# Attention with rings of three PSUM banks for scores and exponents, and its slots unrolled

## The chip, the core and the metric

The kernel runs on one core of a Trainium2 chip. The metric is the device time of one execution in microseconds (us), as the median of several runs. The engines have names in the profile: PE is TensorE (PEld its weight loads), DVE is VectorE, ACT is ScalarE, POOL is GpSimd, and SP is SyncE, whose queue issues the transfers. PSUM, the memory that TensorE writes, has eight banks of 512 f32 values in each of 128 partitions.

## What is computed

Two layers, each of cross attention and a feed-forward part, over 8 batches of 512 rows and 256 features. Both attentions have 16 heads of 16 features:

```
scores = einsum('bqhd,bkhd->bhqk', qp, kp) / sqrt(16)        # layer 0: masked by the mask
scores = where(mask == 0, -10000., scores)                   # layer 1: only j < i is kept
attn   = softmax(scores, axis=-1)
ctx    = einsum('bhqk,bkhd->bqhd', attn, vp) @ Wo.T + Wo_b
```

Layer norms and residuals stand between them. Layer 0 ends with a ternary matmul on quantized rows, layer 1 with a gated feed-forward on quantized rows. Only the two attentions bear on the change.

## The kernel before

The program has four stages: the projections (`project_phase`), the attention of layer 0, that of layer 1 (both `attention_phase`), and the gated feed-forward. The change is in `attention_phase` alone.

An attention is cut into 32 **slots** (8 batches times `G` = 4 groups of four heads) of 16 **steps** `s`. A slot `t` is a software pipeline over three head groups. In step `s` of slot `t` TensorE makes

- one tile of scores of group `t + 2` (`maxima`, L775), from which VectorE takes the negated row maximum (L1161);
- one tile of transposed scores of group `t` with the maximum already subtracted by extra contraction rows (`exponents`, L798), of which ScalarE takes the exponential into `probs` (L986);
- after every fourth step the product of four heads' `probs` with the values (`weigh`, L820), which accumulates in the bank `av`.

At step 5 the maxima of group `t + 1`, split by GpSimd into three bf16 parts (L1052 to L1058), are transposed by TensorE into the bank `max` (`turn_max`, L830). ScalarE copies them out at its step 8 (L998) and SP writes them by DMA into row positions of `q_stack` (L693), for the exponents of the next slot. At step 10 the finished output of group `t - 1`, which ScalarE copied from `av` at step 4 (L992), is transposed into the bank `turn` (`turn_out`, L839). VectorE normalizes it at its step 13 (L1167, L1171).

In layer 1 the tiles are causal. A query tile needs 128, 256, 384 or 512 keys, and each score tile gets a small mask matmul (L778, L801). Narrow tiles share a bank: four of 128 or two of 256 make one **fill**, which is read by one instruction. In layer 0 each step is a fill of its own.

PSUM is shared out as two score banks, two exponent banks, `av`, `turn`, `max` and `work`. TensorE may write fill `n` of the scores when fill `n - 2` has been read, and likewise for the exponents:

```
n = FILLS * t + f
if place == 0 and not (known(t) and n < 2):
    pe.wait_ge(score_read, n - 1)
```

Each engine runs its own instruction stream in order. Within one step the order on TensorE is `maxima`, `exponents`, `weigh`, `turn_max` or `turn_out`, then the after-work of an earlier batch. That after-work (`after`, `queries`, through the bank `work`) is: output projection and residual in the slot that `behind` numbers j = 0, layer norm on VectorE in j = 1, and in layer 0 also the query projection of layer 1 for the batch before (`queries`, L904) in j = 1, the ternary matmul in j = 2 and a second layer norm in j = 3. In layer 1, slots j = 2 and j = 3 have none.

The slots are run by `run`: those from -2 to 11 are written out, 12 to 27 are a hardware loop (`Fori`) of two passes of eight slots, with semaphore values computed in registers (`wait_apart`), and 28 to 40 are written out again.

Of the kernel before, what the change touches and what calls it, by code (L numbers as in the profile page):

```python
# [12 lines left out]
P = 128  # L13
# [11 lines left out]
NSTACK = R_MAX + PARTS  # L25
VW = HD + 1
# [477 lines left out]
def attention_phase(nc, dram, scratch, const, w, layer, stacks, normed=None, tops=None, ffn=None):  # L504
# [22 lines left out]
    with ExitStack() as mem:  # L527
# [52 lines left out]
        out_copied, out_turned, out_normed = sem("out_copied"), sem("out_turned"), sem("out_normed")  # L580
        inverted = sem("inverted")
        max_chain, max_split = sem("max_chain"), sem("max_split")
        max_turned, max_copied = sem("max_turned"), sem("max_copied")
# [83 lines left out]
        def _(sp):  # L667
# [18 lines left out]
            def slot(t, r, i):  # L686
                half, g = (r // G) % 2, r % G
                if there(t, t + 1):
                    u = r + 1
                    wait_apart(sp, max_copied, t + 2)  # L690
# [4 lines left out]
                if not (known(t) and not RING - LEAD <= t <= LAST_LEAD):  # L695
                    n = r + LEAD
                    wait_apart(sp, exp_full, FILLS * (t + LEAD - RING + 1))
# [61 lines left out]
        def _(pe):  # L759
            def program(general):  # L760
                def maxima(t, r, i, s):
# [23 lines left out]
                def exponents(t, r, i, s):  # L785
# [5 lines left out]
                    n = FILLS * t + f  # L791
                    if place == 0 and not (known(t) and n < 2):
                        pe.wait_ge(exp_done, n - 1)
                    q0 = P * kc if causal else 0
                    w = T - q0
                    o = exp_bank[(FILLS * r + f) % 2][:, place * w:(place + 1) * w]
# [13 lines left out]
                def weigh(t, r, i, kc):  # L810

                    half, g = (r // G) % 2, r % G
                    pe.wait_ge(exp_done, FILLS * t + fills_through(kc))
# [10 lines left out]
                def turn_max(t, r):  # L824

                    pe.wait_ge(max_split, t + 1)
                    if not (known(t) and t < 1):
                        pe.wait_ge(max_copied, t)
                    for qt in range(TT):
                        mm = pe.transpose(max_bank[0:PARTS * 4, qt * P:(qt + 1) * P], max_parts[r % 2][:, qt, :, :].rearrange("p a b -> p (a b)"), const["ident_b"][:, :])  # L830
# [983 lines left out]
```

## Time and profile before

| | us |
|---|---|
| median of 3 runs (lowest, highest) | 1672.05 (1665.68, 1674.05) |
| the profiled execution | 1669.25 |
| its span, first to last instruction | 1667.5 |
| slots 1 to 32 of layer 0, from copy to copy of L992 | 477.4 |
| slots 1 to 32 of layer 1, likewise | 402.3 |

A slot is read off the trace from one start of ScalarE's copy `b_out<-b_av` (L992) to the next, since it comes once in a slot. A matmul's own duration overlaps its neighbours': the time that TensorE needs for one is the distance to the next start where nothing is waited for. Durations of VectorE and ScalarE likewise overlap by about 0.1 us where instructions follow each other directly.

### The profile page before, as it was taken

To read this page: it belongs to the slowest core of one execution; us is meant where nothing else is said; L and a number is where in the kernel's file an instruction comes from. 1 tells how busy PE (TensorE), PEld (TensorE's weight loads), DVE (VectorE), ACT (ScalarE), POOL (GpSimd) and SP (SyncE) were. 2 spreads that over 40 slices of the span, in tenths; PEclk is the share of its full clock that TensorE was granted. 3 is DMA by queue.
4 is the path that set the end of the run, shared out by engine and by line. 5 is a ranking of instruction groups with operands and counts; after the bars stand their busy time and mean duration, and the time that the engine had idled before them with its cause. 6 is when DMAs were issued, how large, how long until landed. Compare 5 with 4: busy or idle time off the path is not lost. (4 is left out here: it accounts for less than half of the span.)

```text
span 1667.5 us, 24772 instructions
## 1 busy us (share of the span) xinstructions
PE 1394.5 (84%) x7817; PEld 671.1 (40%) x7829; DVE 1053.0 (63%) x2019; ACT 869.7 (52%) x1488; POOL 219.9 (13%) x335
## 2 busy tenths in 40 slices
PE   8898946999999999997468999998998599970199
PEld 4444411232433433432224554454444344430187
DVE  5434226789889889884367667775674342997832
ACT  4444422766767767765215555554555244868331
POOL 0000000011121221222200000000000000445100
PEclk9999975999999999998759999999999799995599
DMA  7757455123243332333030243233330000315122
GB/s 270 258 187 259 175 167 157 40 85 90 61 114 85 97 116 72 108 103 115 32 102 2 55 115 98 85 86 85 99 83 27 13 0 0 151 76 189 63 89 88
DMA packets 87926, 170.85 MB, mean 102 GB/s; under 512 B 14585, under 2 KB 49156, under 8 KB 86276
## 3 DMA queue, kind: packets, MB, share of 16 engines
q1 hardware_dynamic: 87812, 169.42, 32.0%
q8 instruction: 60, 0.98, 0.3%
q14 instruction: 54, 0.44, 0.1%
HBM read 108.27 MB, written 60.31 MB: 101 GB/s over the span
## 5 line engine op out<-in xcount | busy, mean ns | idle before, releaser
L1161 DVE TENSOR_REDUCE b_neg_max<-b_score 128x1 f32<-128x512 f32 (+3 forms) x864 | 554.0, 665 | 226.1 <-PE b_score L778 127.8
L986 ACT ACTIVATE b_probs<-b_exp 128x512 f32<-128x512 f32 (+1 forms) x864 | 478.3, 582 | 363.6 <-PE b_exp L801 196.3
L775 PE MATMUL b_score<-k_stack,q_stack 97*128 97x512 bf16 (+3 forms) x1024 | 366.2, 359 | 85.9 <-DVE b_neg_max L1161 43.4
L798 PE MATMUL b_exp<-q_stack,k_stack 100*128 100x512 bf16 (+3 forms) x1024 | 352.2, 347 | 22.4 <-DMA q_stack<-b_max_rows 11.6
L775 PEld LDWEIGHTS b_score<-k_stack,q_stack 97*128 97x128 bf16 x1024 | 100.8, 99 | 383.4 <-DVE b_neg_max L1161 276.6
L820 PE MATMUL b_av<-b_probs,values 128*17 128x512 f32 (+3 forms) x2048 | 229.2, 520 | 0.8 <-ACT b_probs L986 0.6
L1687 PE MATMUL f_down<-f_w_downT,f_tmp 128*128 128x256 f32 x384 | 85.9, 388 | 88.4 <-DVE f_tmp L1369 88.4
L1052 POOL CAST b_max_parts<-b_neg_max 128x16 bf16<-128x16 f32 x64 | 14.5, 227 | 1027.4 <-DVE b_neg_max L1161 1027.4
L798 PEld LDWEIGHTS b_exp<-q_stack,k_stack 100*128 100x128 bf16 x1024 | 100.3, 99 | 103.8 <-ACT b_probs L986 40.3
L778 PE MATMUL b_score<-diag_qk,minus_big 128*128 128x128 bf16 x512 | 116.8, 229 | 0.0
L1687 PEld LDWEIGHTS f_down<-f_w_downT,f_tmp 128*128 128x128 f32 x384 | 74.8, 195 | 99.9 <-DVE f_tmp L1369 89.2
L801 PE MATMUL b_exp<-diag_kq,minus_big 128*128 128x128 bf16 x512 | 113.3, 223 | 0.0
L1405 PE MATMUL f_bank<-normed,f_w_upT 128*128 128x512 f32 x192 | 84.2, 595 | 1.1 <-ACT f_up L1472 1.0
L1405 PE MATMUL f_bank<-normed,f_w_gateT 128*128 (+1 forms) x192 | 84.3, 596 | 0.0
L423 DVE TENSOR_TENSOR a_va<-a_bank,bv 128x512 f32<-128x512 f32 x32 | 22.0, 686 | 84.8 <-PE a_bank L261 84.7
L853 PE MATMUL b_work<-wo,b_attendedT 128*128 128x256 f32 x256 | 65.2, 400 | 3.1 <-DVE b_x L1119 1.7
L998 ACT ACTIVATE b_max_rows<-b_max 12x512 bf16<-12x512 bf16 x64 | 36.5, 570 | 59.1 <-PE b_max L830 59.1
L333 ACT ACTIVATE a_part_q<-a_bank 128x512 bf16<-128x512 f32 x48 | 26.8, 594 | 75.1 <-PE a_bank L243 58.7
L241 PE MATMUL a_bank<-a_ctxT,wk 128*128 128x512 f32 x128 | 60.5, 617 | 5.6 <-DMA bk<-L_bk_in 5.5
L1361 ACT ACTIVATE f_tmp<-f_hidden,f_magic,f_inv_prod 128x768 f32 (+2 forms) x32 | 30.2, 1016 | 65.6 <-PE f_down L1687 42.0
L820 PEld LDWEIGHTS b_av<-b_probs,values 128*17 128x17 f32 x2048 | 34.0, 95 | 73.2 <-issue 45.6
L1504 DVE TENSOR_REDUCE f_tops_gate<-f_hidden (+1 forms) x8 | 26.8, 3354 | 57.4 <-ACT f_hidden L1444 57.4
(206 smaller groups left out, 1822.2 us busy)
## 6 DMA issues: line engine op xcount, KB each, us to landing
q_stack<-s_q SPq DMA_DIRECT2D x384, 64.0 KB
s_k<-a_part_k SPq DMA_DIRECT2D x48, 256.0 KB, 4.3
k_stack<-s_k SPq DMA_DIRECT2D x64, 192.0 KB
s_up<-f_up SPq DMA_DIRECT2D x6, 1536.0 KB, 5.1
s_va<-a_va SPq DMA_DIRECT2D x16, 544.0 KB, 4.2
values<-s_va SPq DMA_DIRECT2D x16, 544.0 KB, 3.9
a_mask_q<-mask_in SPq DMA_DIRECT2D x8, 1024.0 KB, 7.4
k_stack<-s_k SPq DMA_DIRECT2D x64, 128.0 KB
```

The costliest lines, as they stand in the source:

```text
L241: mm = pe.matmul(o[:, :], w["w" + n][:, c, m * P:(m + 1) * P], src[:, c, :], start=(c == 0), stop=(c == DC - 1))
L775: mm = pe.matmul(o, q, KS[half][0:R_MAX, h, 0:w], start=True, stop=not general)
L778: mm = pe.matmul(o[:, w - P:w], const["minus_big"][:, :], d[:, :], start=False, stop=True, skip_group_check=True)
L798: mm = pe.matmul(o, k, QS[half][0:NSTACK, h, q0:T], start=True, stop=not general)
L801: mm = pe.matmul(o[:, 0:P], const["minus_big"][:, :], d[:, :], start=False, stop=True, skip_group_check=True)
L820: mm = pe.matmul(av_bank[32 * j:32 * j + VW, q0:T], VA[half][:, kc, 4 * g + j, :], probs[kc][:, j, q0:T], start=(kc == 0), stop=(kc == TT ...
L853: mm = pe.matmul(work[:, x * D:(x + 1) * D], src[:, c, y * P:(y + 1) * P], wt[:, c, :], start=(c == 0), stop=(c == DC - 1))
L986: nc.scalar.activation(probs[kc][:, h0:h0 + m, q0:T], exp_bank[(FILLS * r + f) % 2][:, 0:m * w].rearrange("p (h n) -> p h n", h=m), ACT.Ex ...
L998: nc.scalar.activation(max_rows[u % 2][:, :], max_bank[0:PARTS * 4, 0:T], ACT.Copy).then_inc(max_copied, 1)
L1161: nc.vector.tensor_reduce(neg_max[u][:, qt, h0:h0 + m], score_bank[(FILLS * r + f) % 2][:, 0:m * w].rearrange("p (h n) -> p h n", h=m), AX ...
L1405: mm = pe.matmul(bank[f][:, :], wt[:, c, f * P:(f + 1) * P], xT[:, bass.ds(b, 1), c, :].rearrange("p a n -> p (a n)"), start=(c == 0), sto ...
L1687: mm = pe.matmul(down[2 * half + u][:, j, :], od[half][:, f, t * P:(t + 1) * P], w_downT[:, f, :], start=(f == 0), stop=(f == FC - 1))
```

## The change

1. **Rings of three.** The banks `turn` and `max` go. Scores and exponents get three banks each, and TensorE may write fill `n` when fill `n - 3` has been read.
2. **The transposes become fills.** The transposed maxima are a fill of the exponent ring, issued at step 5 as before and copied out by ScalarE at its step 5 where it was step 8. The transposed outputs are a fill of the score ring, issued at step 10 as before and normalized by VectorE at its step 10 where it was step 13. The semaphores `max_turned`, `max_copied`, `out_turned` and `out_normed` are replaced by counts of `exp_full`, `exp_done`, `score_full` and `score_read`.
3. **Unrolled slots.** All slots from -2 to 40 are written out; every wait is on a constant.

The arithmetic, the number and the shapes of the instructions stay. In `exponents` the same edit as in `maxima` is made with `exp_fill`, `exp_done` and `exp_bank`.

```diff
+RINGS = 3
...
-        score_bank = [pb(f"score{i}", [P, T], F32) for i in range(2)]
-        exp_bank = [pb(f"exp{i}", [P, T], F32) for i in range(2)]
+        score_bank = [pb(f"score{i}", [P, T], F32) for i in range(RINGS)]
+        exp_bank = [pb(f"exp{i}", [P, T], F32) for i in range(RINGS)]
         av_bank = pb("av", [P, T], F32)
-        turn_bank = pb("turn", [P, T], F32)
-        max_bank = pb("max", [P, 2 * T], BF16)
...
+        SLOTS = range(-2, LAST + 10)
+        TURN_MAX, TURN_OUT = 5, 10
+
         def run(eng, slot):
 
-            for r in range(-2, 12):
-                slot(r, r, 0)
-            with eng.Fori(1, NB // 2 - 1) as i:
-                for r in range(4, 12):
-                    slot(8 * i + r, r, i)
-            for r in range(4, 17):
-                slot(LAST - 7 + r, r, NB // 2 - 1)
+            for t in SLOTS:
+                slot(t, t, 0)
+
+        score_fill, exp_fill = {}, {}
+        for t in SLOTS:
+            for s in range(STEPS):
+                f, place, m = fill_of(MAX_FILLS, s)
+                if place == 0 and 0 <= t + 2 <= LAST:
+                    score_fill["max", t + 2, f] = len(score_fill)
+                if s == TURN_OUT and 0 <= t - 1 <= LAST:
+                    score_fill["out", t - 1] = len(score_fill)
+                f, place, m = fill_of(EXP_FILLS, s)
+                if place == 0 and 0 <= t <= LAST:
+                    exp_fill["exp", t, f] = len(exp_fill)
+                if s == TURN_MAX and 0 <= t + 1 <= LAST:
+                    exp_fill["max", t + 1] = len(exp_fill)
...
                 def maxima(t, r, i, s):
...
-                    n = FILLS * t + f
-                    if place == 0 and not (known(t) and n < 2):
-                        pe.wait_ge(score_read, n - 1)
+                    n = score_fill["max", t, f]
+                    if place == 0 and n >= RINGS:
+                        pe.wait_ge(score_read, n - RINGS + 1)
                     w = widths[qt]
-                    o = score_bank[(FILLS * r + f) % 2][:, place * w:(place + 1) * w]
+                    o = score_bank[n % RINGS][:, place * w:(place + 1) * w]
...
                 def turn_max(t, r):
 
+                    n = exp_fill["max", t]
                     pe.wait_ge(max_split, t + 1)
-                    if not (known(t) and t < 1):
-                        pe.wait_ge(max_copied, t)
+                    if n >= RINGS:
+                        pe.wait_ge(exp_done, n - RINGS + 1)
...
-                    mm.then_inc(max_turned, 1)
+                    mm.then_inc(exp_full, 1)
...
                 def turn_out(t, r):
 
+                    n = score_fill["out", t]
                     pe.wait_ge(out_copied, t + 1)
-                    if not (known(t) and t < 1):
-                        pe.wait_ge(out_normed, t)
+                    if n >= RINGS:
+                        pe.wait_ge(score_read, n - RINGS + 1)
...
-                    mm.then_inc(out_turned, 1)
+                    mm.then_inc(score_full, 1)
...
         @block.scalar
...
-                    if s == 8 and there(t, t + 1):
-                        act.wait_ge(max_turned, t + 2)
+                    if s == TURN_MAX and there(t, t + 1):
+                        n = exp_fill["max", t + 1]
+                        act.wait_ge(exp_full, n + 1)
...
         @block.sync
...
-                    wait_apart(sp, max_copied, t + 2)
+                    sp.wait_ge(exp_done, exp_fill["max", t + 1] + 1)
...
         @block.gpsimd
...
-                    pool.wait_ge(max_turned, t)
-                wait_apart(pool, score_read, FILLS * (t + 2))
+                    pool.wait_ge(exp_full, exp_fill["max", t - 1] + 1)
+                pool.wait_ge(score_read, maxima_through(t + 1))
...
         @block.vector
...
-                    if s == 13 and there(t, t - 1):
+                    if s == TURN_OUT and there(t, t - 1):
                         v, g = (r - 1) % 2, (r - 1) % G
-                        got = turn_bank[:, :].rearrange("p (t h e) -> p t h e", t=TT, h=4)
-                        dve.wait_ge(out_turned, t)
+                        n = score_fill["out", t - 1]
+                        got = score_bank[n % RINGS][:, :].rearrange("p (t h e) -> p t h e", t=TT, h=4)
+                        dve.wait_ge(score_full, n + 1)
...
```

ScalarE in layer 0, from the first exponential of query tile group 1 (step 4) of a slot on. Names are tile and buffer number, with the semaphores waited for. Before:

```order
L986 ACTIVATE b0_probs1<-b0_exp0 128x512 [waits b0_av_done,b0_exp_full]
L992 ACTIVATE b0_out1<-b0_av 128x512 [waits b0_out_turned,b0_av_done]
L986 ACTIVATE b0_probs1<-b0_exp1 128x512 [waits b0_exp_full]
L986 ACTIVATE b0_probs1<-b0_exp0 128x512 [waits b0_exp_full]
L986 ACTIVATE b0_probs1<-b0_exp1 128x512 [waits b0_exp_full]
L986 ACTIVATE b0_probs2<-b0_exp0 128x512 [waits b0_av_done,b0_exp_full]
L998 ACTIVATE b0_max_rows1<-b0_max 12x512 [waits b0_max_landed1,b0_max_turned]
L986 ACTIVATE b0_probs2<-b0_exp1 128x512 [waits b0_exp_full]
```

Changed:

```order
L1007 ACTIVATE b0_probs1<-b0_exp1 128x512 [waits b0_av_done,b0_exp_full]
L1013 ACTIVATE b0_out1<-b0_av 128x512 [waits b0_score_full,b0_av_done]
L1007 ACTIVATE b0_probs1<-b0_exp2 128x512 [waits b0_exp_full]
L1020 ACTIVATE b0_max_rows1<-b0_exp0 12x512 [waits b0_max_landed1,b0_exp_full]
L1007 ACTIVATE b0_probs1<-b0_exp1 128x512 [waits b0_exp_full]
L1007 ACTIVATE b0_probs1<-b0_exp2 128x512 [waits b0_exp_full]
L1007 ACTIVATE b0_probs2<-b0_exp0 128x512 [waits b0_av_done,b0_exp_full]
L1007 ACTIVATE b0_probs2<-b0_exp1 128x512 [waits b0_exp_full]
```

The copy to `b0_max_rows` stands two exponentials further ahead and reads a bank of the exponent ring, so that the two exponentials behind it use the two banks that are left.

VectorE in layer 0, around the normalization in the same kind of slot. Before:

```order
L1161 TENSOR_REDUCE b0_neg_max1<-b0_score0 128x1 [waits b0_score_full]
L1161 TENSOR_REDUCE b0_neg_max1<-b0_score1 128x1 [waits b0_score_full]
L1161 TENSOR_REDUCE b0_neg_max1<-b0_score0 128x1 [waits b0_score_full]
L1161 TENSOR_REDUCE b0_neg_max1<-b0_score1 128x1 [waits b0_score_full]
L1167 RECIPROCAL b0_inv_sum0<-b0_turn 128x16 [waits b0_out_turned]
L1171 TENSOR_TENSOR b0_attended0<-b0_turn,b0_inv_sum0 128x4x64 [waits b0_inverted]
L1161 TENSOR_REDUCE b0_neg_max1<-b0_score0 128x1 [waits b0_score_full]
```

Changed:

```order
L1184 TENSOR_REDUCE b0_neg_max1<-b0_score1 128x1 [waits b0_score_full]
L1184 TENSOR_REDUCE b0_neg_max1<-b0_score2 128x1 [waits b0_score_full]
L1191 RECIPROCAL b0_inv_sum0<-b0_score0 128x16 [waits b0_score_full]
L1195 TENSOR_TENSOR b0_attended0<-b0_score0,b0_inv_sum0 128x4x64 [waits b0_inverted]
L1184 TENSOR_REDUCE b0_neg_max1<-b0_score1 128x1 [waits b0_score_full]
L1184 TENSOR_REDUCE b0_neg_max1<-b0_score2 128x1 [waits b0_score_full]
```

The two instructions on the transposed output moved ahead by two reductions, and their operand is now a bank of the score ring, between two fills of it.

## Rows read from the trace of the kernel before

**Rows 1.** The page: the span and the engines' busy time over it.

```profile
span 1667.5 us, 24772 instructions
...
PE 1394.5 (84%) x7817; PEld 671.1 (40%) x7829; DVE 1053.0 (63%) x2019; ACT 869.7 (52%) x1488; POOL 219.9 (13%) x335
```

**Rows 2.** Busy time by stretch: layer 0 without after-work, then j = 0, 1, 2, 3.

```profile
core 0: us, PE busy (x) PEld busy (x) DVE busy (x) ACT busy (x) POOL busy (x), PEclk, DMA share, GB/s
313.12:326.94 13.82, 13.24 (x75) 3.71 (x73) 10.71 (x19) 9.83 (x20) 0.84 (x4) 1.00 0.22 59
543.99:560.92 16.93, 16.75 (x99) 7.81 (x96) 13.23 (x26) 10.83 (x22) 4.88 (x6) 1.00 0.40 123
497.53:514.28 16.75, 16.75 (x91) 6.13 (x88) 15.09 (x41) 12.75 (x26) 3.25 (x5) 1.00 0.27 80
514.28:529.02 14.74, 14.01 (x87) 4.99 (x84) 13.16 (x26) 11.24 (x22) 2.92 (x5) 1.00 0.30 81
529.02:543.99 14.97, 13.71 (x79) 4.14 (x76) 13.75 (x39) 10.32 (x20) 3.77 (x6) 1.00 0.38 107
```

**Rows 3.** The same view, layer 1: written-out slot, j = 0, 1, 2, loop boundary.

```profile
1016.76:1029.00 12.24, 11.39 (x108) 5.66 (x106) 7.35 (x14) 6.66 (x14) 0.83 (x4) 1.00 0.41 102
1041.19:1055.94 14.75, 14.49 (x128) 9.08 (x124) 10.09 (x24) 7.19 (x15) 0.84 (x4) 1.00 0.25 73
1055.94:1068.54 12.60, 11.36 (x108) 5.55 (x105) 11.11 (x31) 6.67 (x15) 0.83 (x4) 1.00 0.37 107
1068.54:1080.76 12.22, 11.30 (x108) 5.60 (x105) 7.28 (x14) 6.66 (x14) 0.83 (x4) 1.00 0.27 72
1120.34:1138.21 17.87, 12.99 (x104) 6.29 (x101) 7.13 (x14) 6.88 (x15) 0.83 (x4) 0.84 0.32 88
```

**Rows 4.** Timeline (start, duration), layer 0: one group of steps on PE.

```profile
319.58 0.38 PE L775 MATMUL b_score<-k_stack,q_stack 97*128 97x512 bf16 x1
...
319.80 0.38 PE L798 MATMUL b_exp<-q_stack,k_stack 100*128 100x512 bf16 x1
...
320.31 0.39 PE L775 MATMUL b_score<-k_stack,q_stack 97*128 97x512 bf16 x1
...
320.91 0.39 PE L775 MATMUL b_score<-k_stack,q_stack 97*128 97x512 bf16 x1
...
321.45 1.05 PE L820 MATMUL b_av<-b_probs,values 128*17 128x512 f32 x8
...
322.43 0.39 PE L775 MATMUL b_score<-k_stack,q_stack 97*128 97x512 bf16 x1
```

**Rows 5.** Timeline, layer 0: runs of reductions and of exponentials without waits between.

```profile
312.41 2.58 DVE L1161 TENSOR_REDUCE b_neg_max<-b_score 128x1 f32<-128x512 f32 x4 [0.81 <-PE b_score L775]
...
323.08 1.09 ACT L986 ACTIVATE b_probs<-b_exp 128x512 f32<-128x512 f32 x2 [0.93 <-PE b_exp L798]
```

**Rows 6.** Timeline of PE, layer 0: after-work, each with what starts next.

```profile
501.06 1.88 PE L904 MATMUL b_work<-b_xT,wq 128*128 128x512 f32 x4
...
502.78 0.38 PE L775 MATMUL b_score<-k_stack,q_stack 97*128 97x512 bf16 x1
...
510.60 0.60 PE L845 MATMUL b_work<-ident_f,b_xn 128*128 128x128 f32 x4
...
511.04 0.38 PE L775 MATMUL b_score<-k_stack,q_stack 97*128 97x512 bf16 x1
```

**Rows 7.** Timeline of PE, layer 1: matmuls that came late.

```profile
1069.57 0.34 PE L798 MATMUL b_exp<-q_stack,k_stack 100*128 100x384 bf16 x1 [0.16 <-ACT b_probs L986]
...
1074.76 0.22 PE L801 MATMUL b_exp<-diag_kq,minus_big 128*128 128x128 bf16 x1
1075.26 0.39 PE L775 MATMUL b_score<-k_stack,q_stack 97*128 97x512 bf16 x1 [0.28 <-DVE b_neg_max L1161]
...
1078.48 0.39 PE L798 MATMUL b_exp<-q_stack,k_stack 100*128 100x512 bf16 x1 [0.26 <-ACT b_probs L986]
```

**Rows 8.** Timeline of PE, layer 1, at the loop's boundary.

```profile
1133.09 0.28 PE L775 MATMUL b_score<-k_stack,q_stack 97*128 97x128 bf16 x1 [4.32 <-issue]
```

More of the change, by code:

```diff
@@ L790, in exponents @@
                     f, place, m = fill_of(EXP_FILLS, s)
-                    n = FILLS * t + f
-                    if place == 0 and not (known(t) and n < 2):
-                        pe.wait_ge(exp_done, n - 1)
+                    n = exp_fill["exp", t, f]
+                    if place == 0 and n >= RINGS:
+                        pe.wait_ge(exp_done, n - RINGS + 1)
                     q0 = P * kc if causal else 0
                     w = T - q0
-                    o = exp_bank[(FILLS * r + f) % 2][:, place * w:(place + 1) * w]
+                    o = exp_bank[n % RINGS][:, place * w:(place + 1) * w]
                     k = KS[half][0:NSTACK, h, kc * P:(kc + 1) * P]
@@ L874, in after @@
                         if n == 0:
-                            pe.wait_ge(out_normed, G * (b + 1))
+                            pe.wait_ge(score_read, score_fill["out", G * (b + 1) - 1] + 1)
                         mm = turn(att[half], n)
@@ L919, in slot @@
                                 weigh(t, r, i, s // 4 - 1)
-                        if s == 5 and there(t, t + 1):
+                        if s == TURN_MAX and there(t, t + 1):
                             turn_max(t + 1, r + 1)
-                        if s == 10 and there(t, t - 1):
+                        if s == TURN_OUT and there(t, t - 1):
                             turn_out(t - 1, r - 1)
@@ L989, in slot @@
                         act.wait_ge(av_done, 4 * t)
-                        if not (known(t) and t < 3):
-                            act.wait_ge(out_turned, t - 2)
+                        if t >= 3:
+                            act.wait_ge(score_full, score_fill["out", t - 3] + 1)
                         nc.scalar.activation(out_sb[(r - 1) % 2][:, :], av_bank[:, :], ACT.Copy).then_inc(out_copied, 1)
-                    if s == 8 and there(t, t + 1):
-                        act.wait_ge(max_turned, t + 2)
+                    if s == TURN_MAX and there(t, t + 1):
+                        n = exp_fill["max", t + 1]
+                        act.wait_ge(exp_full, n + 1)
                         u = r + 1
@@ L1158, in slot @@
                         if place == m - 1:
[L1159 removed]
+                            n = score_fill["max", t + 2, f]
+                            dve.wait_ge(score_full, n + 1)
                             h0, w = s % 4 - place, widths[qt]
[L1161 removed]
+                            nc.vector.tensor_reduce(neg_max[u][:, qt, h0:h0 + m], score_bank[n % RINGS][:, 0:m * w].rearrange("p (h n) -> p h n", h=m),
                                                     AX.X, ALU.max, negate=True).then_inc(score_read, 1)
[L1163 removed]
+                    if s == TURN_OUT and there(t, t - 1):
                         v, g = (r - 1) % 2, (r - 1) % G
[L1165 to L1166 removed]
+                        n = score_fill["out", t - 1]
+                        got = score_bank[n % RINGS][:, :].rearrange("p (t h e) -> p t h e", t=TT, h=4)
+                        dve.wait_ge(score_full, n + 1)
                         nc.vector.reciprocal(inv_sum[v][:, :, :], got[:, :, :, HD]).then_inc(inverted, 1)
@@ L1171, in slot @@
                         nc.vector.tensor_tensor(att[(r - 1) // G % 2][:, :, 4 * HD * g:4 * HD * (g + 1)].rearrange("p t (h d) -> p t h d", h=4),
-                                                got[:, :, :, 0:HD], spread, ALU.mult).then_inc(out_normed, 1)
+                                                got[:, :, :, 0:HD], spread, ALU.mult).then_inc(score_read, 1)
                     if layer == 1 and known(t) and t < 4 and s in (3, 8, 13):
```

26 lines of the change are left out of this document (15 added, 11 removed).

## Prediction

> **What bounds the kernel now.** I read the page first: TensorE is busy for 84% of the span, VectorE for 63%, ScalarE for 52% [rows 1]. Since matmul durations overlap, that does not say that TensorE is full. So I read one slot of each kind as a stretch: in layer 0 a slot without after-work takes 13.82 us with VectorE busy for 10.71 and ScalarE for 9.83, and one of layer 1 takes 12.22 with 7.28 and 6.66 [rows 2, 3]. No engine fills them. The granted clock is 1.00 in both, the upper level of 2.4 GHz, so the clock is not what is lost. Then the timeline of TensorE. Back to back, a 512-column matmul is followed by the next after 0.22 us (319.58 to 319.80) and a `weigh` after 0.98 (321.45 to 322.43) [rows 4]. Next to that stand holes. After the exponent tile at 319.80, which is over at 320.02, the third score tile comes at 320.31: 0.29 lost. The pair from 320.31 is over at 320.75, the fourth score tile comes at 320.91: 0.16 lost. These are waits for a score bank. VectorE does four reductions in a row in 2.58 us, so one each 0.63 (the last lasts 0.69), and two exponentials take 1.09, one each 0.5 [rows 5]. TensorE makes a pair in 0.44, so four pairs outrun VectorE, and it catches up during `weigh`. Two banks are too few for this unevenness, not for the average.
>
> **What a slot needs.** Layer 0: 32 tiles x 0.22 = 7.04, four `weigh` x 0.98 = 3.92, `turn_max` and `turn_out` 0.76 together (four transposes of f32 take 0.44, 510.60 to 511.04 [rows 6]; I take 0.32 for the bf16 ones, an estimate), and about 0.09 before each `weigh` that no bank removes (320.91 plus 0.44 is 321.35, it starts at 321.45 [rows 4]), 0.36. Sum 12.1 of 13.82: 1.7 us of holes in a base slot.
>
> **Part 1, three banks for scores.** Worked for four steps with VectorE at the start idle: tiles at 0, 0.44, 0.88, and the fourth needs the first read, at 0.43 + 0.63 + 0.1 = 1.16, before 1.32. No hole, where it was 0.45. `weigh` ends at 2.83, VectorE's four reductions at 2.96: it is nearly full within a group, and has `turn_out`'s group and `turn_max`'s group to catch up. Its whole work per base slot, 16 x 0.63 + 0.7 = 10.8, stays below 12.1. So all score holes of a base slot go.
>
> **Part 2, the transposes as fills.** The output transpose takes a place in the score ring between the third and fourth tile of its group. VectorE holds that bank for about 0.7 us more. With tiles at 0, 0.44, 0.88, transpose 1.32, fourth tile 1.76, VectorE is through the third at 2.3, the normalization at 3.05, the fourth tile at 3.7; the tile that needs the transpose's bank again comes at 3.7. No hole. The transposed maxima take a place in the exponent ring in the group where ScalarE also copies the output. Its order becomes exponential, output copy, exponential, maxima copy, then two exponentials. The fourth exponent tile of that group needs the second one's bank, which is free after 0.65 + 0.5 + 0.47 + 0.6 = 2.2 us, the same as with two banks and a separate one. So the hole of about 0.3 in this group **stays**: three banks less one fill are two. The same hole stands in layer 1 at 1069.57, with 0.16 shown idle and as much hidden in the modelled durations [rows 7]. This part costs nothing else: GpSimd waits for the same events; SP's wait for the maxima copy stands in the same place of its queue and comes true about 2 us earlier, and the stack transfers queued behind it with it; the DMA engines are busy for 0.22 to 0.41 of a slot [rows 2, 3].
>
> A base slot of layer 0 thus goes from 13.8 to 12.5: **1.3** saved (1.7 less 0.3, and 0.1 for rest). There are four intervals of this kind (slots 1 to 5): 5.2.
>
> **Slots with after-work, layer 0.** j = 1 adds two `turn` (0.88) and two query projections x 1.72 (501.06 to 502.78 [rows 6]), 4.3: needs 16.4 of 16.75, and TensorE is full: 0.4 saved. j = 0 adds as many f32 columns: 16.4 of 16.93, 0.5. j = 2 needs 13.4 of 14.74, but VectorE is busy for 13.16: 1.0. j = 3 needs 12.5 of 14.97, and VectorE is busy for 13.75, with a whole layer norm between reductions: what it can win is its idle 1.2 and one more fill of lead (0.63) less what it leaves idle in any case; I take 1.3 [rows 2]. Seven intervals of the first three kinds and six of the last: 7 x 1.9 + 6 x 1.3 = 21. With the last two intervals (1.5) layer 0 saves **28**.
>
> **Layer 1.** In the slot 1068.54 to 1080.76 late tiles stand six times: from 1069.57 (ScalarE) over 1075.26 (VectorE; the tile before starts at 1074.76 and needs 0.06, so 0.44 lost with 0.28 shown) to 1078.48 (ScalarE) [rows 7]. By their kinds: 1.1 in the two groups with wide score tiles (VectorE), 0.5 in the group with the wide exponents (ScalarE), 0.3 in the `turn_max` group, which stays as above. So a slot without after-work saves 1.6. j = 1 (12.60, VectorE busy 11.11) is bound by VectorE's layer norm for most of its length: 1.0. j = 0 has one hole of 0.4 and small ones: 0.6 [rows 3]. The first four intervals, which share VectorE with the weight quantization, 1.0 each. Sum: 4 + 7 x 0.6 + 7 x 1.0 + 13 x 1.6 + 1.5 = **37.5**.
>
> **Part 3, unrolled.** At the loop's only back edge in layer 1, slot 19 to 20, TensorE stands still for 4.32 us with nothing to wait for, and the matmuls behind it run at a lower clock: that slot took 17.87 us, with a granted clock of 0.84, where its kind takes 12.2 [rows 3, 8]. Without the loop this goes: **5.6**. Straight code costs nothing visible: slots 1 to 11 and 28 on are written out already, and a written-out one takes 12.24 where one in the loop takes 12.22 [rows 3]. The registers' arithmetic was hidden, too, by the same two rows. What I can't see is only whether 43 slots in a row behave as 14 do.
>
> A rule of the Trainium skill speaks against this part. The trace shows that TensorE loses 4.32 us at one jump and none in written-out slots [rows 3, 8]. "Advanced Engine Details and Errata", section "ISA Cache", gives TensorE 128 KB in lines of 256 instructions, with two lines; code that is run once is then fetched line by line, where a loop that fits is kept. By it, unrolling trades one late fetch for many, and if they came late the kernel would be slower; the written-out slots speak for fetches that come in time.
>
> **Sum.** 28 + 37.5 + 5.6 = 71 off the profiled execution's 1669.25: 1598. The median of the runs is 2.8 above that execution, so **1601** for the median. The stages outside the attentions, and the tail of layer 0 after slot 32, stay.
>
> **Rivals.** (a) The third bank gives half. For it: VectorE is busy for 11.11 to 15.09 us in all slots with a norm, and a lead of three fills makes `turn_max` wait for the split maxima, which need the last reduction and four GpSimd steps. Against: base slots have no such work. Then 65 / 2 + 5.6 = 38 off: 1634. (b) The rings give nothing, since the new fills take the third bank's place and what is left is a ring of two: only the back edge goes, and 1666 comes out. For it: that is so in the `turn_max` group. Against: the transposes are one fill in 17 in layer 0 and one in 12 in layer 1. (c) **Slower**: code fetch. If straight code past the first slots stalled as the back edge does, 4.32 us each, then 17 stalls would eat all 71. TensorE runs over 100 matmuls and weight loads in a slot [rows 2]; with a stall in each of the 2 x 16 slots that come out of the loops, 32 x 4.32 = 138 less 71 is 67 more: 1739. Against: [rows 3] as above.
>
> **Chances.** Forecast 0.66, (a) 0.22, (b) 0.07, (c) 0.05. The range is 1588 (VectorE's bound in the norm slots is softer than I took: 1 us more in each of 13) to 1640, which takes in (a). About 0.5% is what a measurement of this kernel can tell from no change; so faster 0.88, same 0.07, slower 0.05.
>
> **What would show it.** Right: a base slot of layer 0 at 12.5 and one of layer 1 at 10.6; four tiles in a row at 0.44 in groups without `turn_max`; the hole before the fourth exponent tile in the `turn_max` group still there; slot 19 to 20 of layer 1 like its neighbours; j = 1 of layer 0 almost unchanged. Wrong: reductions that wait while TensorE waits at `turn_max` (a), holes of the old size (b), or stops with no releaser at places spread over the slots (c).

## The result, and the profile after

The changed kernel takes **1608.9 us** (median of four runs, 1608.38 to 1609.36), beside 1668.97 for the kernel before on the same chip: a ratio of 0.9637, 95% interval 0.9607 to 0.9668. That is 7.9 us above the 1601 forecast and inside its range. The saving is 60.1 us, where 71 was forecast: the kernel before also reads 3.1 us less here than the 1672.05 that the forecast started from. Its profiled execution has a span of 1606.7 us, 60.8 less than before.

The page of the changed kernel, to be read against [rows 1]: the same work, with busy times within some 2% of before, in a shorter span.

```profile
span 1606.7 us, 22090 instructions
...
PE 1364.4 (85%) x7829; PEld 673.5 (42%) x7829; DVE 1043.9 (65%) x2019; ACT 850.1 (53%) x1488; POOL 221.5 (14%) x335
```

Busy time by stretch in the changed kernel, one slot each, answering to [rows 2]: layer 0 without after-work, j = 0, 1, 2, 3, and one of the two long j = 3 slots.

```profile
core 0: us, PE busy (x) PEld busy (x) DVE busy (x) ACT busy (x) POOL busy (x), PEclk, DMA share, GB/s
308.10:320.64 12.54, 12.39 (x75) 3.81 (x73) 10.62 (x19) 9.27 (x19) 0.84 (x4) 1.00 0.24 65
533.52:550.09 16.57, 16.57 (x99) 7.90 (x97) 12.69 (x24) 10.56 (x21) 5.11 (x6) 1.00 0.26 80
488.00:504.55 16.55, 16.55 (x91) 6.27 (x89) 15.39 (x42) 12.45 (x25) 3.26 (x5) 1.00 0.28 82
504.55:518.10 13.55, 13.55 (x87) 5.15 (x85) 12.28 (x23) 10.93 (x21) 2.94 (x5) 1.00 0.33 98
518.10:533.52 15.42, 13.58 (x79) 3.96 (x77) 14.44 (x41) 10.09 (x21) 3.52 (x6) 1.00 0.50 142
392.89:409.33 16.44, 14.91 (x79) 4.31 (x77) 14.57 (x41) 10.08 (x20) 4.14 (x6) 0.90 0.36 116
```

The first is 12.54, where 12.5 was forecast and 13.82 stood. The j = 3 slot is the one that did not go as said: 15.42 and 16.44, where 14.97 stood.

The same view of layer 1, answering to [rows 3]: j = 0, j = 1, and the j = 2 slot 19 to 20, which was the loop's boundary.

```profile
1002.42:1016.52 14.10, 14.10 (x124) 8.99 (x123) 9.35 (x19) 6.84 (x16) 0.84 (x4) 1.00 0.25 74
1016.52:1028.30 11.78, 11.03 (x104) 5.47 (x102) 11.34 (x36) 6.35 (x14) 0.53 (x3) 1.00 0.37 114
1076.17:1086.92 10.75, 10.37 (x106) 5.78 (x107) 7.11 (x14) 6.38 (x14) 1.09 (x6) 1.00 0.39 114
```

What TensorE waited for, over the whole span (engine, line, releaser: us in total, times, longest). Before:

```profile
PE b_score L775 <- DVE b_neg_max L1161: 43.4, 110, 5.5
PE b_score L775 <- issue: 25.5, 2, 21.1
...
PE b_exp L798 <- ACT b_probs L986: 9.0, 38, 0.6
```

After:

```profile
PE b_score L792 <- issue: 20.7, 1, 20.7
PE b_score L792 <- DVE b_neg_max L1184: 17.8, 40, 4.9
...
PE b_exp L815 <- ACT b_probs L1007: 1.4, 6, 0.5
```

The waits for a score bank fell from 43.4 to 17.8 us (3.8 more are new, `turn_out` at L859 waiting for one) and those for an exponent bank from 9.0 to 1.4. These sums understate what was lost: a tile is reported with 0.38 us and its successor can start after 0.22, so the first 0.16 of a wait behind a tile is not seen as idle. "issue" came twice and comes once: the one that is gone was the loop's jump, the other lies outside the slots.

By kind of slot, both traces, each sum over the intervals from copy to copy (before, after, what was saved, and what the prediction's terms say for the same intervals):

| | count | before | after | saved | forecast |
|---|---|---|---|---|---|
| layer 0, first four | 4 | 55.26 | 50.61 | 4.7 | 5.2 |
| layer 0, j = 0, 1, 2 | 18 | 291.37 | 280.10 | 11.3 | 13.3 |
| layer 0, j = 3 | 6 | 89.79 | 94.55 | **-4.8** | **7.8** |
| layer 0, last three | 3 | 41.01 | 40.03 | 1.0 | 1.5 |
| layer 1, first four | 4 | 57.36 | 48.02 | 9.3 | 4 |
| layer 1, j = 0 | 6 | 88.06 | 84.58 | 3.5 | 3.6 |
| layer 1, j = 1 | 6 | 75.37 | 70.71 | 4.7 | 6 |
| layer 1, j = 2, 3 and the jump | 12 | 152.49 | 131.57 | 20.9 | 24.8 |
| layer 1, last three | 3 | 29.00 | 27.74 | 1.3 | 4.7 |
| between slot 32 and slot 1 of layer 1 | 1 | 104.27 | 97.95 | 6.3 | 0 |
| before slot 1 of layer 0, after the last | | | | 2.8 | 0 |

(Where the prediction counted seven intervals of a kind and six stand in a row, the seventh's share is with "last three" in layer 1; in layer 0 it is in the 13.3. Of the 11.3 saved in the second row, 1.66 is no merit of the change: one j = 2 slot of the profiled execution before, 577.67 to 594.07, lasted 16.40 where its kind takes 14.74.)

### The profile page after: what moved, and what is told of

The parts are those of the page before. It is cut to its first block and busy times, and to the rows that moved or that the text cites. A ratio compares the mean times of both kernels' runs of the same rounds, so it can differ in the third digit from the quotient of the medians.

```text
span 1606.7 us, 22090 instructions
## 1 busy us (share of the span) xinstructions
PE 1364.4 (85%) x7829; PEld 673.5 (42%) x7829; DVE 1043.9 (65%) x2019; ACT 850.1 (53%) x1488; POOL 221.5 (14%) x335
## 5 line engine op out<-in xcount | busy, mean ns | idle before, releaser
L1184 DVE TENSOR_REDUCE b_neg_max<-b_score 128x1 f32<-128x512 f32 (+3 forms) x864 | 545.8, 664 | 177.7 <-PE b_score L795 89.4
L1007 ACT ACTIVATE b_probs<-b_exp 128x512 f32<-128x512 f32 (+1 forms) x864 | 463.9, 581 | 325.7 <-PE b_exp L818 164.0
L815 PE MATMUL b_exp<-q_stack,k_stack 100*128 100x512 bf16 (+3 forms) x1024 | 347.6, 343 | 18.8 <-DMA q_stack<-b_max_rows 15.9
L815 PEld LDWEIGHTS b_exp<-q_stack,k_stack 100*128 100x128 bf16 x1024 | 100.5, 99 | 96.5 <-ACT b_probs L1007 22.7
L1020 ACT ACTIVATE b_max_rows<-b_exp 12x512 bf16<-12x512 bf16 x64 | 36.6, 572 | 56.7 <-PE b_exp L849 56.7
L242 PE MATMUL a_bank<-a_ctxT,wk 128*128 128x512 f32 x128 | 60.8, 619 | 5.6 <-DMA bk<-L_bk_in 5.6
```

What stands on the lines that cost most here:

```text
L242: mm = pe.matmul(o[:, :], w["w" + n][:, c, m * P:(m + 1) * P], src[:, c, :], start=(c == 0), stop=(c == DC - 1))
L815: mm = pe.matmul(o, k, QS[half][0:NSTACK, h, q0:T], start=True, stop=not general)
L1007: nc.scalar.activation(probs[kc][:, h0:h0 + m, q0:T], exp_bank[n % RINGS][:, 0:m * w].rearrange("p (h n) -> p h n", h=m), ACT.Exp).then_in ...
L1020: nc.scalar.activation(max_rows[u % 2][:, :], exp_bank[n % RINGS][:, :].bitcast(BF16)[0:PARTS * 4, 0:T], ACT.Copy).then_inc(exp_done, 1)
L1184: nc.vector.tensor_reduce(neg_max[u][:, qt, h0:h0 + m], score_bank[n % RINGS][:, 0:m * w].rearrange("p (h n) -> p h n", h=m), AX.X, ALU.ma ...
```

## The experiments

All of them start from the changed kernel, except the first, which starts from the kernel before. "Base slot" is one of layer 0 without after-work: 13.82 before, 12.54 after. A ratio is the median over that of the kernel before, taken beside the run. Beside the three groups of runs the kernel before read 1668.6, 1667.4 and 1666.9, so a difference of two medians from different groups is good to some 2 us.

### The parts of the change: unrolled alone, and rings of two

The slots of the kernel before, written out, nothing else:

```diff
...
-            with eng.Fori(1, NB // 2 - 1) as i:
-                for r in range(4, 12):
-                    slot(8 * i + r, r, i)
...
+            for t in range(-2, LAST + 10):
+                slot(t, t, 0)
```

> The kernel before with its attention slots written out and nothing else. If unrolling gives what the sum took for it, slot 19 to 20 of layer 1 falls from 17.9 to 12.3 us and nothing else moves: 5.6 us off, ratio 0.9966. If straight code costs fetches, it comes out at the time of before or over it, with stops spread over the slots. If the 6 us between the two layers and the 4 us ahead of layer 0 that the changed kernel saved came from straight code, they show here too: 15 us off.

Measured: 1659.08, ratio 0.9942 (0.9923 to 0.9961), 9.9 us less than 1668.97 and 9.5 less than the 1668.59 beside it. Slot 19 to 20 of layer 1, in its trace:

```profile
1117.65:1129.74 12.09, 11.25 (x106) 5.61 (x105) 7.28 (x14) 6.67 (x14) 0.84 (x4) 1.00 0.38 108
```

17.87 became 12.09 [rows 3], so 5.8 is the jump, as forecast. The slots of layer 0 are as before to 0.1 us (13.81, 16.99, 16.71, 14.74, 14.94), but for the odd one of 16.40, which is 14.74 here. In layer 1 the slots that were in the loop went from 14.75 to 14.51 (j = 0) and from 12.60 to 12.49 (j = 1), about 2 us in all: the arithmetic on registers was nearly hidden, not wholly. Slot 1 of layer 0 began 3.1 us earlier, but that start moves between 295.3 and 300.5 from kernel to kernel with no pattern that I can read, so I count it to nobody.

The changed kernel with two banks in each ring:

```diff
-RINGS = 3
+RINGS = 2
```

> The changed kernel with rings of two banks, the transposes being fills of these. If a third bank is what gives, and a fill that takes one of two banks costs, base slots of layer 0 are above 13.8 us and the kernel is slower than before less 5.6, about 1690 us. If the transposes as fills cost nothing, slots are as before: 1663 us.

Measured: 1693.82, ratio 1.0159 (1.0131 to 1.0188). A base slot:

```profile
313.94:328.51 14.57, 13.51 (x72) 3.60 (x72) 10.80 (x19) 9.94 (x20) 0.83 (x4) 1.00 0.23 56
```

So the change is three parts of very different size: written out -9.9; transposes into the rings +34.7 (1659.08 to 1693.82); third banks -84.9 (1693.82 to 1608.9). The middle step also moves the two copies out of these fills ahead on ScalarE and VectorE, as in the change, and no run with two banks separates the two; nor do slots account for all of the first, of which 5.8 is the jump and some 2 the registers. The prediction had the middle one at nothing, since it looked at it only together with the third bank. Rival (b) had its mechanism right and its size wrong: the fills eat 0.76 of the 2.0 us that the third banks give in a base slot.

### Which of the two third banks counts

`RINGS` split into a size for each ring, 3 and 2, then 2 and 3:

```diff
-RINGS = 3
+SCORE_RING, EXP_RING = 3, 2
...
```

> The changed kernel with three score banks and two exponent banks (one PSUM bank unused). Rings of two on both sides made a base slot of layer 0 14.57 us, rings of three 12.54. If the holes were those of VectorE's side alone, as the prediction's row of a group says, most of the 2.0 us comes from the scores' third bank and this kernel's base slot is 13.0 or less, the kernel near 1625 us. If the exponents' third bank is needed to make up for the maxima's place in that ring, base slots are 13.8 or more and the kernel is no faster than before: 1660 us or over.

> The changed kernel with two score banks and three exponent banks, the fourth case beside 2/2 (base slot of layer 0 14.57), 3/2 (13.68) and 3/3 (12.54). If both sides' holes are at different places of a slot and add, the base slot is 14.57 less 1.14 = 13.43 and the kernel near 1650 us. If the holes of one side hide behind those of the other, it is above 13.8: 1665 us or over.

Measured: 1641.91, ratio 0.9846 (0.9805 to 0.9886), with three score banks; 1659.52, ratio 0.9946 (0.9925 to 0.9967), with three exponent banks. A base slot of the first, then of the second:

```profile
314.22:327.90 13.68, 13.05 (x72) 3.76 (x72) 10.71 (x19) 9.71 (x19) 0.84 (x4) 1.00 0.24 60
```

```profile
313.84:327.97 14.13, 13.48 (x75) 3.38 (x73) 10.71 (x19) 9.81 (x20) 0.84 (x4) 1.00 0.21 58
```

| score banks / exponent banks | 2 / 2 | 3 / 2 | 2 / 3 | 3 / 3 |
|---|---|---|---|---|
| base slot, layer 0 | 14.57 | 13.68 | 14.13 | 12.54 |
| median | 1693.8 | 1641.9 | 1659.5 | 1608.9 |

In the base slot one bank alone saves 0.89 or 0.44, both together 2.03: 0.7 us of the waits go only when both sides have their third bank. That freeing one side shows the other's waits is how I read it, and the rows of waits below fit. My expectation of 13.43 for the 2 / 3 slot took the savings as a sum and was wrong. Over the whole kernel, though, they do nearly add up (51.9 and 34.3, together 84.9), as only the four base slots and j = 2 of layer 0 show much of it (j = 2: 0.86 and 0.41 alone, 1.59 together; j = 0 of layer 1: 0.18 and 1.02 alone, 1.20 together). The waits moved to the side that kept two banks. With two exponent banks:

```profile
PE b_exp L849 <- ACT b_probs L1007: 20.7, 61, 0.6
PE b_score L792 <- DVE b_neg_max L1184: 13.6, 29, 5.4
```

With two score banks:

```profile
PE b_score L792 <- DVE b_neg_max L1184: 40.3, 106, 6.8
```

The exponents' side (L815) waits for 0.8 us there.

### Why j = 3 of layer 0 became longer

First suspicion: `turn_out` as a score fill at step 10, amid the layer norm. Moved to step 13, where VectorE took it before the change:

```diff
-        TURN_MAX, TURN_OUT = 5, 10
+        TURN_MAX, TURN_OUT = 5, 13
```

> The changed kernel with the output transposes and the normalization at step 13 in place of 10. Theory: in slots j = 3 of layer 0 the 0.7 us of normalization fall into the steps (5 to 12) in which VectorE does a whole layer norm, TensorE's waits bunch there, and the clock falls in some of them. Then j = 3 slots fall from 15.4 and 16.4 to about 14.9 us, none has a granted clock under 1.00, about 6 us off the changed kernel: 1603 us. Rival: VectorE's total work bounds j = 2 and j = 3 together, wherever it stands: 1609 us.

Measured: 1610.02, ratio 0.9654 (0.9626 to 0.9682): no gain. All six j = 3 slots now take 15.71, so the place of the fill moves them by 0.3, and is not why they are long.

Second: VectorE itself. TensorE in the long slot, timeline of the changed kernel (start, duration, idle before it in brackets):

```profile
396.86 0.39 PE L792 MATMUL b_score<-k_stack,q_stack 97*128 97x512 bf16 x1 [0.44 <-DVE b_neg_max L1184]
397.08 0.38 PE L815 MATMUL b_exp<-q_stack,k_stack 100*128 100x512 bf16 x1
398.01 0.63 PE L859 MATMUL b_score<-ident_f,b_out 128*128 128x128 f32 x4 [0.55 <-DVE b_neg_max L1184]
398.99 0.39 PE L792 MATMUL b_score<-k_stack,q_stack 97*128 97x512 bf16 x1 [0.35 <-DVE b_neg_max L1184]
```

VectorE over the same time:

```profile
396.12 0.68 DVE L1184 TENSOR_REDUCE b_neg_max<-b_score 128x1 f32<-128x512 f32 x1
396.71 0.15 DVE L1124 TENSOR_TENSOR b_square<-b_rstd 128x4 f32<-128x4 f32 x1
396.90 0.16 DVE L1126 SCALAR_TENSOR_TENSOR b_square<-b_square,b_var 128x4 f32<-128x4 f32 x1
397.10 0.16 DVE L1128 SCALAR_TENSOR_TENSOR b_rstd<-b_square,b_rstd 128x4 f32<-128x4 f32 x1
397.18 0.68 DVE L1184 TENSOR_REDUCE b_neg_max<-b_score 128x1 f32<-128x512 f32 x1
```

A step costs VectorE 1.06 here (396.12 to 397.18): the reduction, 0.63 by itself, and three instructions of the layer norm's inverse root on four values. They start 0.2 apart and add 0.43 together, since the next reduction starts 0.08 after the last of them. TensorE needs 0.44 for the pair and a quarter of a `weigh`, some 0.7. If VectorE is the bound over the whole stretch, more banks can't help and less work on VectorE must; no run has more than three banks, and the next one takes work away. It leaves out the last two Newton steps of the root (six of twelve instructions, so the norms are less exact):

```diff
-        NROOT = 12
+        NROOT = 6
```

> The changed kernel with 6 in place of 12 small VectorE instructions for each layer norm's inverse root: the last two of the three Newton steps are left out, so its norms are less exact. It takes 1.2 us (6 x 0.2) off VectorE in slots j = 1 and j = 3 of layer 0 and j = 1 of layer 1. Theory: j = 3 of layer 0 is bound by VectorE from its step 0 to 12, so it falls from 15.4 to 14.3 us or less, without slots of 16.4 or a clock under 1.00; j = 1 of layer 0, full on TensorE, stays at 16.55; j = 1 of layer 1 falls from 11.78 to about 11.2. 17 us off the changed kernel: 1592 us. Rival: TensorE waits in j = 3 for the order of ring places and not for VectorE's work: within 3 us of 1609.

Measured: 1592.36, ratio 0.9557 (0.9517 to 0.9597), 16.5 less than the changed kernel. The same j = 3 slot:

```profile
514.66:529.15 14.49, 13.46 (x79) 3.96 (x77) 13.65 (x35) 10.09 (x20) 3.52 (x6) 1.00 0.49 127
```

15.42 became 14.49 and 16.44 too (0.93 for six instructions, about 0.15 each); j = 0, 1 and 2 of layer 0 stayed (16.57, 16.55, 13.55), and j = 1 of layer 1, which also has a norm, went from 11.78 to 11.03. VectorE is the bound there, and there only.

Why longer than before the change, when VectorE's work is the same? Its reductions over j = 2 and j = 3 together, before (514.28 to 543.99) and after (504.55 to 533.52): count, busy, mean ns, idle before them.

```profile
L1161 DVE TENSOR_REDUCE b_neg_max<-b_score 128x1 f32<-128x512 f32 x33 | 21.9, 683 | 2.5 <-PE b_score L775 2.4
```

```profile
L1184 DVE TENSOR_REDUCE b_neg_max<-b_score 128x1 f32<-128x512 f32 x33 | 21.6, 683 | 1.9 <-PE b_score L792 1.8
```

From the reduction at 507.58 to 532.1 VectorE now waits for nothing, over the border at 518.10:

```profile
507.58 2.00 DVE L1184 TENSOR_REDUCE b_neg_max<-b_score 128x1 f32<-128x512 f32 x3 [0.67 <-PE b_score L792]
...
527.76 4.37 DVE L1184 TENSOR_REDUCE b_neg_max<-b_score 128x1 f32<-128x512 f32 x7
532.81 1.29 DVE L1184 TENSOR_REDUCE b_neg_max<-b_score 128x1 f32<-128x512 f32 x2 [0.67 <-PE b_score L792]
```

The two slots took 29.71 and take 28.97 together. There were only 2.5 us of idle to win in the pair and 0.6 was won. j = 2 became 1.2 shorter, so that TensorE reaches j = 3 earlier, with VectorE no further: the time won in one was handed back in the other. The count of reductions that start in each shows it: 15 and 17 before, 14 and 18 after, so one of 0.63 us went over the border.

### The root on GpSimd

GpSimd is busy for 3.52 of a j = 3 slot, so the root can go there, as 14 small instructions of GpSimd in place of VectorE's 12 (the same three Newton steps; the first guess is made with a product by -0.5 where VectorE shifts, and a step takes four instructions for three). These lines stand in GpSimd's `slot`, in the first kernel ahead of `split`, in the second at its end, with `inverse_root` moved from VectorE's block to GpSimd's. In both VectorE's scalings by the root, and the clipping behind them, stand one step later:

```diff
+                if j in ((1, 3) if layer == 0 else (1,)) and is_batch(b):
+                    for n in range(NROOT):
+                        inverse_root(NLN * b + j // 2, n)
```

> The changed kernel with each layer norm's inverse root moved from VectorE to GpSimd (14 small instructions in place of 12, about 0.28 us each by the split's rows, 4 us in all), the scalings one step later. VectorE loses 2.4 us of work in slots j = 1 and j = 3 of layer 0 and j = 1 of layer 1. Theory: j = 3 of layer 0 is VectorE's and falls to 13.2 to 13.6, j = 1 of layer 1 from 11.78 to 11.0, j = 1 of layer 0 stays: 25 us off the changed kernel: 1584 us. Rival: VectorE waits at step 10 for the slower chain with its reductions queued behind, and j = 1 slots of layer 0 and 1 get longer: 1600 us or over.

> The kernel e8_pool_root with GpSimd's 14 small instructions at the end of its slot's work and not ahead of the split of the maxima. In e8 the split, which TensorE's transpose at step 5 needs, stood behind a wait for the norm's statistics of step 4 of the same slot, and slots with a norm took 18 to 25 us. Theory: that order was all of it; now j = 3 of layer 0 takes 13.2 to 13.8 us (15.42 in the changed kernel), j = 1 of layer 1 about 11.0 (11.78), j = 1 of layer 0 16.5, 20 us off the changed kernel: 1589 us. Rival: the chain takes over 4 us, VectorE waits for it at step 10 with its reductions queued behind, and it comes out at 1600 us or over.

Measured: ahead of the split 1750.29, ratio 1.0500 (1.046 to 1.054), and the slots with a norm last 20 to 25.5 us in layer 0 (in part at a lower clock: 0.77 to 0.91 is granted over them). What TensorE waits for says why:

```profile
PE b_exp L849 <- POOL b_max_parts L1103: 123.0, 28, 6.4
```

GpSimd stands at the root's first instruction until the norm's variance comes (371.9 us over 24 times), the split stands behind it, and `turn_max` and all of TensorE behind the split. At the end of GpSimd's work it is 1586.98, ratio 0.9527 (0.9497 to 0.9557), 21.9 less than the changed kernel. The same j = 3 slot, 13.26 where it was 15.42:

```profile
513.92:527.18 13.26, 13.00 (x79) 4.20 (x77) 12.78 (x29) 9.94 (x20) 5.97 (x20) 1.00 0.44 116
```

VectorE is busy for 12.78 in place of 14.44, and GpSimd for 5.97. The move has a small price in two other kinds of slot. j = 1 of layer 0 went from 16.55 to 16.86, where 16.5 was expected: TensorE's transpose of the normalized rows (L865) comes 0.28 later there. j = 2 of layer 1 went from 10.75 to 11.08, where `turn_max` waits for 0.73 for the split and waited for 0.47.

### The hole in the `turn_max` group

The prediction said that a hole of 0.3 before the fourth exponent tile of this group stays. It does. PE and ACT in a base slot of the changed kernel:

```profile
308.10 0.59 ACT L1013 ACTIVATE b_out<-b_av 128x512 f32<-128x512 f32 x1
308.58 0.60 ACT L1007 ACTIVATE b_probs<-b_exp 128x512 f32<-128x512 f32 x1
308.70 0.38 PE L792 MATMUL b_score<-k_stack,q_stack 97*128 97x512 bf16 x1
309.06 0.57 ACT L1020 ACTIVATE b_max_rows<-b_exp 12x512 bf16<-12x512 bf16 x1
309.24 0.39 PE L815 MATMUL b_exp<-q_stack,k_stack 100*128 100x512 bf16 x1 [0.15 <-ACT b_probs L1007]
```

The exponent tile could follow the score tile at 308.92 and comes at 309.24, when the exponential of 308.58 has been read out. Moving `turn_max` to step 7 puts ScalarE's two copies apart; in a second kernel ScalarE also makes its after-work copy ahead of the maxima copy in that step.

```diff
-        TURN_MAX, TURN_OUT = 5, 10
+        TURN_MAX, TURN_OUT = 7, 10
```

```diff
+                    if is_batch(b):
+                        after(b, j, s)
+                    if layer == 0 and earlier(b):
+                        queries(b - 1, j, s)
                     if s == TURN_MAX and there(t, t + 1):
...
-                    if is_batch(b):
-                        after(b, j, s)
-                    if layer == 0 and earlier(b):
-                        queries(b - 1, j, s)
```

> The changed kernel with the transposed maxima at step 7 in place of 5, on TensorE and ScalarE. Theory: the hole of 0.3 us that stays in the group of the maxima comes from ScalarE's order exponential, output copy, exponential, maxima copy. With the copy behind the fourth exponential it goes: base slots of layer 0 from 12.54 to 12.25 and of layer 1 from 10.76 to 10.45, about 14 us off in all: 1595 us. Rival: the wait moves to the group behind, or the maxima's transfer lands too late for the next slot: 1609 us or over.

> The kernel e4_max7 with ScalarE's copy of the maxima behind the after-work's copy of step 7 and not ahead of it. In e4 slots with after-work became longer (layer 1, j = 0: 14.10 to 14.57; layer 0, j = 0 to 2: plus 0.2). Theory: that is ScalarE waiting for the maxima at step 7 with the copy of the turned output, which the output projection at step 9 needs, queued behind. Then these slots are back at 14.1 or less and 16.55 or less, and the 0.5 us of the base slots are kept: 1592 us. Rival: the extra time is the transposes' place on TensorE itself: 1600 us.

Measured: 1600.31, ratio 0.9598 (0.9571 to 0.9624), then 1589.36, ratio 0.9539 (0.9502 to 0.9576). A base slot of layer 0 in the first, and a j = 0 slot of layer 1:

```profile
310.38:322.39 12.01, 12.01 (x74) 4.00 (x72) 10.52 (x19) 9.35 (x20) 0.84 (x4) 1.00 0.25 68
951.86:966.43 14.57, 14.31 (x127) 9.26 (x127) 9.35 (x19) 6.92 (x16) 0.84 (x4) 1.00 0.30 88
```

The base slot gave up 0.53, more than the hole of 0.32 and more than the 0.3 expected; the hole is gone in the trace, and the other 0.2 has no experiment. But the slots in which ScalarE has an after-work copy at step 7 lost (14.10 to 14.57 here, 16.57 to 16.75 in layer 0). With that copy first they are 14.09 and 16.31: the order of two instructions on ScalarE was worth 11 us. Both together with the root at GpSimd's end:

> The kernels e7_max7_late and e9_pool_root_last in one: maxima at step 7, inverse roots on GpSimd. Theory: the one takes 0.3 to 0.6 us off slots bound by ScalarE's order and TensorE, the other 1 to 2 us off slots bound by VectorE, in different slots, so the gains add: 20 and 20 off the changed kernel, 1570 us. Rival: with GpSimd's chain the maxima, split later, hold up step 7: no better than e7, 1589 us.

Measured: **1562.61** (1561.7 to 1565.08), ratio 0.9385 (0.9366 to 0.9404). A base slot, a j = 3 slot of layer 0 and a j = 1 slot of layer 1:

```profile
307.28:319.29 12.01, 12.01 (x74) 3.99 (x72) 10.53 (x19) 9.35 (x20) 0.84 (x4) 1.00 0.24 68
507.10:520.56 13.46, 13.04 (x79) 4.61 (x80) 12.82 (x29) 10.16 (x20) 6.00 (x20) 1.00 0.35 84
936.29:946.64 10.35, 10.21 (x107) 5.83 (x106) 9.55 (x24) 6.53 (x15) 3.14 (x16) 1.00 0.32 80
```

46 us below the changed kernel and 106 below the one before. In the base slot PE is busy from end to end.

## Why the prediction was right, and where it was not

- **Base slot of layer 0, 12.5.** 12.54, three times of four; the fourth, 12.98, already has other neighbours. Tiles stand 0.44 apart (314.29, 314.72, 315.16 for the score tiles of a group). The experiments with rings of two and three show that the third banks did it. The mechanism is right in part: the prediction laid all holes but one to the score banks, yet with a third bank there alone the slot is 13.68, 0.13 less than before. The exponents' third bank, which it took only as room for the maxima's fill, is needed for the other 1.14.
- **The hole that stays.** Shown above at 309.24, 0.32 long; with `turn_max` at step 7 it is gone and the slot is 12.01.
- **Slots with a norm and a transpose, j = 0, 1, 2 of layer 0.** Right within 0.2 each: 16.57, 16.55, 13.55 for 16.4, 16.4 and 13.7.
- **j = 3 of layer 0, the step that failed.** "What it can win is its idle 1.2 and one more fill of lead ... I take 1.3" gave 6 x 1.3 = 7.8. It was -4.8, and 12.6 us of the miss; 2.0 of them are the lower clock in two of the six slots (last section), the other four alone became 0.44 longer each. The slot was taken by itself. But VectorE's stretch without slack runs over the border from j = 2, so the savings of the two are no sum: the pair had 2.5 us of idle before the reductions, of which 0.6 went, and I had booked 2.3. VectorE as the bound is shown by the run with half the root, in which j = 3 of layer 0 and j = 1 of layer 1 react and the other kinds don't, and by the run with the root on GpSimd. The first j = 1 slot of layer 0, slot 6 to 7, reacts too: it went from 15.86 to 17.04 (15.57 with half the root), of which some 0.5 is the clock (16.49 to 16.51 in three kernels with the whole root in which the clock stays).
- **Layer 1, j = 0 and j = 1.** 0.6 and 0.8 each, for 0.6 and 1.0. Just behind j = 1 rival (a)'s wait shows, at 1028.74, `[0.47 <-POOL b_max_parts L1080]` before `turn_max`: a mechanism that is there, for 5.7 us over 8 times in the whole span.
- **Layer 1, j = 2 and 3.** 10.76 and 11.16 for 10.6 and 10.6: 15.1 without the jump, for 19.2 forecast. Of the 1.6 a slot, j = 3 gave 1.1. Its end holds the start of the next j = 0, as the copy that marks the border comes at step 4; that this is why is argued, not shown.
- **First slots of layer 1 and the stretch ahead of them.** Booked at 4 and at nothing, they gave 9.3 and 6.3. With two banks nothing of it shows, neither in the unrolled kernel (first slots 58.5, between the layers 105.98) nor in the changed kernel with rings of two (56.7 and 105.06), so it is the third banks, and mostly the scores': with three score banks alone 51.2 and 99.2, with three exponent banks alone 55.1 and 105.96. (The stretch between the layers moves by itself: 101.35 with `turn_out` at step 13.) The first slots were mis-sized because I took VectorE as full there without reading a row for it.
- **Unrolled, 5.6.** 5.8 for the jump, 9.9 in all. The prediction took the registers' arithmetic as hidden; it was not wholly so: the written-out j = 0 slots of layer 1 before took 14.52, those in the loop 14.75. Rival (c) did not come: no slot of either unrolled kernel has a stop of TensorE over 0.1 us without a releaser, in 43 slots in a row; only the jump back was late. "Advanced Engine Details and Errata" of the Trainium skill, section "ISA Cache", gives the size and the lines of TensorE's instruction cache and no cost. That it speaks against straight code was the prediction's inference, and these traces don't bear it out.
- **Sum.** Too high in layer 0 by 15.6, and in layer 1's slots by 3.5; too low between the layers and at the ends by 9. Of what was too high, 3.0 is a slip of the sum: 4 intervals and 7 + 7 + 7 + 6 are already all 31 of a layer, and the 1.5 for "the last two intervals" was added to each layer on top. The forecast came near by luck in part: misses of both signs met, and the kernel before read 3.1 us less than when the forecast was made.

Not settled: what brings the lower clock (last section), why the start of slot 1 moves by some us between kernels, and why the fills in rings of two cost what they do in each kind of slot (against the unrolled kernel 0.76 in a base slot of layer 0, 0.86 in j = 3, 0.40 in j = 2).

## What to carry to other kernels

Size a ring of banks against every producer and consumer at once: one side's third bank can show a fraction of its worth until the other side has one too (0.89 and 0.44 against 2.03 in the base slots here, though over the whole kernel the two nearly add), and whatever else is put into the ring costs a part of it. Where an engine is full over a border of stages, add up its idle time over the whole full stretch and book no more than that, however the savings look stage by stage. When such an engine is found, small instructions on few values are the first to move, behind everything in the other queue that someone waits for, and never ahead of it.

## What the hardware showed beyond that

Three slots of the changed kernel were granted a mean clock of 0.90 and lasted 0.5 to 1.0 us longer than their kind (17.04, 16.44, 16.43). Busy time in steps of 2 us in the second of them, then in the j = 3 slot of 15.42 (the last three columns are the granted clock, the DMA share and GB/s):

```profile
396.00:398.00 2.00, 1.03 (x4) 0.14 (x3) 1.86 (x8) 1.58 (x3) 0.00 (x0) 1.00 0.18 64
398.00:400.00 2.00, 1.64 (x10) 0.66 (x14) 1.97 (x6) 0.46 (x2) 0.00 (x0) 0.86 0.44 137
400.00:402.00 2.00, 2.00 (x10) 0.28 (x3) 1.68 (x5) 0.23 (x1) 0.00 (x0) 0.50 0.75 196
...
522.00:524.00 2.00, 1.24 (x6) 0.53 (x6) 1.86 (x9) 0.92 (x2) 0.00 (x0) 1.00 0.35 100
524.00:526.00 2.00, 1.80 (x12) 0.41 (x13) 1.97 (x7) 0.60 (x1) 0.00 (x0) 1.00 0.26 78
```

After TensorE had waited three times for VectorE (0.44, 0.55 and 0.35, the rows above), its granted clock fell to 0.50, the lower level of 1.2 GHz (the upper is 2.4), with TensorE busy for 2.00 of 2.00 us, and the slot took 16.44 where 15.42 is usual. But the usual slot has the same three waits (0.43 at 522.07, 0.54 at 523.22, 0.35 at 524.20) at a granted clock of 1.00, and so have the three others of 15.41. So the waits alone don't bring the fall, and what does is open. Where it falls, 1.0 us is lost. No slot of layer 0 falls under 1.00 in the runs with `turn_out` at step 13, `turn_max` at step 7, half the root, or the root at the end of GpSimd's work. And in the kernel before one slot had 588 to 590 us with TensorE busy for 0.33 and VectorE for 0.43 and no cause that the trace shows (it puts VectorE's wait down to GpSimd's split, which was over 0.96 us before the wait ended): single slots of one execution should not carry an argument.
